# Inverse roots of row and head norms as a power on GpSimd, in place of a root on ScalarE and a reciprocal on VectorE

## The reference

```python
def _layernorm(x, axis=-1, eps=1e-05):
    m = jnp.mean(x, axis=axis, keepdims=True)
    v = jnp.var(x, axis=axis, keepdims=True)
    return (x - m) / jnp.sqrt(v + eps)

# layer A: delta-rule memory with 16 heads of 8, convolutions, two linear scans over time
q = q * jax.lax.rsqrt(jnp.sum(q * q, axis=-1, keepdims=True) + 1e-12)
# layer B: binding in the frequency domain
fk = fk / (jnp.abs(fk) + EPS)

# layer F: causal attention with 16 heads of 8, then 4 experts, 2 chosen per row
def _rms(x, w):
    return x * jax.lax.rsqrt(jnp.mean(x * x, axis=-1, keepdims=True) + EPS) * w
h = _rms(x, n1_w)
q = _rms(heads(wq), qn_w)
k = _rms(heads(wk), kn_w)
...
causal = jnp.tril(jnp.ones((T, T), bool))
```

## Time and profile before

| | us |
|---|---|
| median of 3 runs | 1208.35 (1207.23 to 1209.22) |
| the profiled execution's own time | 1207.07 |
| its span in the trace | 1205.2 |

### The profile page before, as it was taken

The page is one execution under the profiler, slowest core; times in us unless marked ns, Lnnn a source line. Parts: engine busy times, 40 slices in busy tenths (PEclk is TensorE's granted clock), DMA queues, the critical chain, the costliest instruction groups (busy, mean ns, idle before and its releaser), DMA issues.

```text
span 1205.2 us, 11485 instructions
## 1 busy us (share of the span) xinstructions
PE 674.5 (56%) x4014; PEld 333.1 (28%) x4014; DVE 867.5 (72%) x1306; ACT 506.5 (42%) x752; POOL 403.4 (33%) x334
## 2 busy tenths in 40 slices
PE   4990000040004004479899799963264799978997
PEld 2450000040004003222222556631243122225655
DVE  6899999999999995856657733269959557667212
ACT  3423000122220001579999322243034899973321
POOL 1250847600006602226765000006802566650000
PEclk9985555555555556779999799987565899997999
DMA  2250006172000020223310000000003242100001
GB/s 92 70 140 1 1 0 140 35 168 63 13 14 14 0 35 0 84 75 116 97 33 22 1 1 1 1 0 1 0 0 115 63 142 54 54 1 1 1 1 35
DMA packets 30258, 50.71 MB, mean 42 GB/s; under 512 B 4472, under 2 KB 14328, under 8 KB 29176
## 3 DMA queue, kind: packets, MB, share of 16 engines
q1 hardware_dynamic: 29432, 49.32, 15.2%
q10 hardware_dynamic: 768, 0.66, 0.3%
HBM read 20.98 MB, written 16.92 MB: 31 GB/s over the span
## 4 chain that ended last, share of the span: by engine, by line
DVE 47%; PE 23%; ACT 16%; issue 10%; POOL 1%; DMA 1%; ACTq 1%; POOLq 0%; SPq 0%; DVEq 0%
ACT PX L1445 10%; PE PS L1330 6%; PE PS L1308 5%; PE PS L1350 4%; PE PS L1289 3%; DVE D L813 2%; DVE S L817 2%; DVE P L814 2%; DVE PS L871 2%; DVE PRD L870 2%; DVE mag L1031 2%; DVE PA L772 2%; ACT P L688 2%; DVE RO L837 2%; DVE RP L832 2%
## 5 line engine op out<-in xcount | busy, mean ns | idle before, releaser
L1445 ACT ACTIVATE PX<-PS 128x1024 f32<-128x1024 f32 (+1 forms) x320 | 268.1, 1016 | 12.1 <-PE PS L1271 12.1
L1224 POOL TENSOR_TENSOR PX<-PX,maskf 128x256 f32<-128x256 f32 (+1 forms) x192 | 173.4, 931 | 125.0 <-ACT PX L1445 124.5
L1289 PE MATMUL PS<-PX,VA 128*32 128x512 f32 (+3 forms) x1536 | 166.2, 503 | 22.3 <-POOL PX L1224 14.5
L1617 DVE SCALAR_TENSOR_TENSOR X<-PS,wts,X 128x96 f32<-128x96 f32 x128 | 38.4, 315 | 118.2 <-PE PS L1350 103.9
L1271 PE MATMUL PS<-QS,KS 64*128 64x512 bf16 (+3 forms) x768 | 107.8, 339 | 16.7 <-issue 11.4
L1554 DVE RECIPROCAL DEN<-DEN 128x512 f32<-128x512 f32 x32 | 107.3, 3353 | 1.1
L580 PE MATMUL PS<-ones,HT 64*128 64x1 f32 x64 | 13.0, 348 | 152.0 <-ACT HT L672 152.0
L947 POOL TENSOR_TENSOR PRQ<-PA,LQK 128x2048 f32<-128x2048 f32 (+15 forms) x16 | 39.9, 2520 | 151.8 <-DMA WS<-S 138.6
L1552 DVE LOAD_MASK_SELECT DEN<-PS x32 | 0.4, 14 | 107.2 <-PE PS L1289 93.5
L591 PE MATMUL PS<-awout,V 64*128 64x128 f32 x64 | 13.3, 422 | 110.5 <-DVE vss L820 110.5
L1308 PE MATMUL PS<-HT,fw 128*128 128x512 f32 x144 | 71.2, 638 | 3.9 <-DVE HG L1584 2.6
(11 more groups left out here) (264 smaller groups left out, 1649.5 us busy)
## 6 DMA issues: line engine op xcount, KB each, us to landing
QS<-qs_d SPq DMA_DIRECT2D x32, 196.0 KB
qs_d<-QP SPq DMA_DIRECT2D x24, 256.0 KB, 3.9
ks_d<-QP SPq DMA_DIRECT2D x24, 256.0 KB, 4.0
KS<-ks_d SPq DMA_DIRECT2D x32, 192.0 KB
K<-LQK SPq DMA_DIRECT2D x16, 256.0 KB
W<-WS SPq DMA_DIRECT2D x16, 256.0 KB, 4.1
qkv_d<-CY SPq DMA_DIRECT2D x3, 1024.0 KB, 3.9
LQK<-qkv_d SPq DMA_DIRECT2D x8, 256.0 KB, 4.9
```

Source lines behind the costliest of these rows:

```text
L1224: pool.tensor_tensor(block, block, bcast(maskf[:], 1, 2 * halves), ALU.mult).then_inc(probs_masked, 1)
L1289: last = pe.matmul(PS[32 * h:32 * h + 32, SCORES_BANKS + qc, c0:CH], VA[b][:, kt, h, :], px[:, i % 2, at:at + CH - c0], start=(kt == 0), s ...
L1445: act.activation(tile(PX[u % PDEPTH][:]), tile(PS[:, k:k + 2, :]), ACT.Exp).then_inc(probs_ready, 1)
```

## The change

Two semaphores are added: `to_power` from VectorE to GpSimd and `powered` back. For the norm ahead of all four layers, for q and k and the score bound in both F layers, and for the norm ahead of the experts, the request goes to GpSimd, which writes `stat ** -0.5` (or `qst ** 0.5` for the bound) with one `tensor_tensor` of the operation `pow`; the exponent is a value of the new tile `HALVES`, repeated. ScalarE's roots and VectorE's reciprocals at these places go. The roots of `SS`, `vss`, `SS4` and `mag` stay as they were.

```diff
+        HALVES = sb("HALVES", [P, 2])
...
         def dve_norm(v, link, ans, eps, dst, rms_eps=None):
 
-            v.tensor_scalar(stat[:], mv[:, :, 1], eps, None, ALU.add).then_inc(to_act, 1)
+            v.tensor_scalar(stat[:], mv[:, :, 1], eps, None, ALU.add).then_inc(to_power, 1)
             ans.wait()
-            link(v.reciprocal(rstd[:], stat[:]))
...
+        def pool_power(pool, ask, dst, src, exponent):
+            ask.wait()
+            pool.tensor_tensor(dst, src, exponent, ALU.pow).then_inc(powered, 1)
...
-        def a_gpsimd(pool, link):
+        def a_gpsimd(pool, link, pask):
+            link.open(pool.memset(HALVES[:, 0:1], -0.5))
+            link(pool.memset(HALVES[:, 1:2], 0.5))
             pool.memset(ones[:], 1.0).then_inc(ones_set, 1)
+            pool_power(pool, pask, rstd[:], stat[:], bcast(HALVES[:, 0], 1, TILES))
...
-        def b_gpsimd(pool, link):
+        def b_gpsimd(pool, link, pask):
+            pool_power(pool, pask, rstd[:], stat[:], bcast(HALVES[:, 0], 1, TILES))
...
-        def f_gpsimd(pool, link, nth, rep):
+        def f_gpsimd(pool, link, pask, nth, rep):
+            pool_power(pool, pask, rstd[:], stat[:], bcast(HALVES[:, 0], 1, TILES))
+            pool_power(pool, pask, rrms[:], stat[:], bcast(HALVES[:, 0], 1, TILES))
             if rep == 0:
...
+            def unit_power(b):
+                tb = slice(b * TB, (b + 1) * TB)
+                pool_power(pool, pask, qst2[:, tb], qst[:, tb], bcast(bcast(HALVES[:, 0], 1, 2 * H), 1, TB))
+
+            def root(b):
+                at = qst[:, b * TB:(b + 1) * TB, H:2 * H]
+                pool_power(pool, pask, at, at, bcast(bcast(HALVES[:, 1], 1, H), 1, TB))
+
+            unit_power(0)
+            root(0)
+            unit_power(1)
             for c in range(NCH // B):
                 pool.wait_ge(psum_read, FIRST_RESULT[nth] + NCH + TILES + 2 + 2 * (c + 1))
                 third(pool, c).then_inc(third_parts, 1)
+            root(1)
...
+            for b in range(B):
+                tb = slice(b * TB, (b + 1) * TB)
+                pool_power(pool, pask, rrms[:, tb], stat[:, tb], bcast(HALVES[:, 0], 1, TB))
...
             def q_k_normed(b):
...
-                ans.wait()
-                link(v.reciprocal(qst2[:, tb], qst[:, tb]))
+                pans.wait()
                 link(v.tensor_tensor(to, qk, bcast(qst2[:, tb], 3, HD), ALU.mult))
...
-                v.tensor_scalar(stat[:, tb], stat[:, tb], 1.0 / D, F_EPS, ALU.mult, ALU.add).then_inc(to_act, 1)
-                ans.wait()
-                link(v.reciprocal(rrms[:, tb], stat[:, tb]))
+                v.tensor_scalar(stat[:, tb], stat[:, tb], 1.0 / D, F_EPS, ALU.mult, ALU.add).then_inc(to_power, 1)
+                pans.wait()
```

More of the change, by code:

```diff
@@ L264, in hybrid_kernel @@
         to_act = sem("to_act")
+        to_power = sem("to_power")
+        powered = sem("powered")
         normed = sem("normed")
@@ L396, in dve_norm @@
                 link(v.tensor_tensor(var[:], var[:], rstd[:], ALU.mult))
-                v.tensor_scalar(stat[:], var[:], rms_eps, None, ALU.add).then_inc(to_act, 1)
+                v.tensor_scalar(stat[:], var[:], rms_eps, None, ALU.add).then_inc(to_power, 1)
                 ans.wait()
-                link(v.reciprocal(rrms[:], stat[:]))
                 link(v.tensor_tensor(rrms[:], rrms[:], rstd[:], ALU.mult))
@@ L605, in a_scalar @@
         def a_scalar(act, link, ask, reads):
-            act_sqrt(act, ask, stat[:])
             act_ht(act, reads)
@@ L701, in hybrid_kernel, with a_vector @@
         READ_TURNS = [(0,), (1, 2), (3, 4), (5, 6), (7, 8, 9), (10, 11), (12, 13), (14, 15)]
-        def a_vector(v, link, ans):
+        def a_vector(v, link, ans, pans):
             v.wait_ge(x_loaded, 48)
             dve_stats(v, link, range(TILES))
-            dve_norm(v, link, ans, LN_EPS, XL)
+            dve_norm(v, link, pans, LN_EPS, XL)
             v.wait_ge(a_loaded, 112)
@@ L1010, in b_scalar, with b_vector @@
                     act_sqrt(act, ask, mag[c % 2][0:NB])
-        def b_vector(v, link, ans, nth):
+        def b_vector(v, link, ans, pans, nth):
             v.wait_ge(x_ready, nth)
-            dve_norm(v, link, ans, LN_EPS, XL)
+            dve_norm(v, link, pans, LN_EPS, XL)
             v.wait_ge(normed, B * (FIRST_NORM[nth] + 1))
@@ L1397, in f_scalar @@
                 act.activation(QKV[:, t, :], PS[:, k, 0:3 * D], ACT.Copy).then_inc(psum_read, 1)
-                if t == TB + TPC - 1:
-                    act_sqrt(act, ask, qst[:, 0:TB])
             def q_squares(b):
@@ L1403, in q_squares @@
                 act.activation(QQ[b], QKS[:, b * TB:(b + 1) * TB, 0:D], ACT.Square).then_inc(q_squared, 1)
-            def q_root(b):
-                act_sqrt(act, ask, qst[:, b * TB:(b + 1) * TB, H:2 * H])
             def high(c):
@@ L1422, in f_scalar @@
             high(0)
-            q_root(0)
             high(1)
-            act_sqrt(act, ask, qst[:, TB:2 * TB])
             shifts(0)
@@ L1431, in f_scalar @@
             high(2)
-            q_root(1)
             high(3)
@@ L1446, in f_scalar @@
             for b in range(B):
-                act_sqrt(act, ask, stat[:, b * TB:(b + 1) * TB])
                 act_ht(act, reads, range(b * (NCH // B), (b + 1) * (NCH // B)), HT_BANKS)
@@ L1473, in w_vector, with f_vector @@
             link(v.tensor_scalar(fqk[:, 0], fqk[:, 0], HD ** -0.5, None, ALU.mult))
-        def f_vector(v, link, ans, nth, rep):
+        def f_vector(v, link, ans, pans, nth, rep):
             base = FIRST_RESULT[nth]
@@ L1479, in f_vector @@
                 v.sem_inc(o_read, OBANKS)
-            dve_norm(v, link, ans, LN_EPS, SQ, F_EPS)
+            dve_norm(v, link, pans, LN_EPS, SQ, F_EPS)
             def q_k_squares(b):
@@ L1486, in q_k_squares @@
                 link(v.tensor_reduce(qst[:, tb], to, AX.X, ALU.add))
-                v.tensor_scalar(qst[:, tb], qst[:, tb], 1.0 / HD, F_EPS, ALU.mult, ALU.add).then_inc(to_act, 1)
+                v.tensor_scalar(qst[:, tb], qst[:, tb], 1.0 / HD, F_EPS, ALU.mult, ALU.add).then_inc(to_power, 1)
             def q_k_normed(b):
@@ L1505, in q_k_normed @@
                 v.tensor_reduce(qst[:, tb, H:2 * H], QQ[b].rearrange("p t (h d) -> p t h d", d=HD),
-                                AX.X, ALU.add).then_inc(to_act, 1)
-                ans.wait()
+                                AX.X, ALU.add).then_inc(to_power, 1)
+                pans.wait()
                 link(v.tensor_scalar(qst[:, tb, H:2 * H], qst[:, tb, H:2 * H], HD ** 0.5, -SHIFT, ALU.mult, ALU.add))
@@ L1687, in _ @@
         def _(v):
-            link, ans = Chain(v, dve_chain), Tally(v, to_dve)
+            link, ans, pans = Chain(v, dve_chain), Tally(v, to_dve), Tally(v, powered)
             for n, layer in enumerate(LAYERS):
                 if layer == "A":
-                    a_vector(v, link, ans)
+                    a_vector(v, link, ans, pans)
                 elif layer == "B":
-                    b_vector(v, link, ans, n)
+                    b_vector(v, link, ans, pans, n)
                 else:
-                    f_vector(v, link, ans, n, LAYERS[:n].count("F"))
+                    f_vector(v, link, ans, pans, n, LAYERS[:n].count("F"))
         @block.gpsimd
         def _(pool):
-            link = Chain(pool, pool_chain)
+            link, pask = Chain(pool, pool_chain), Tally(pool, to_power)
             for n, layer in enumerate(LAYERS):
                 if layer == "A":
-                    a_gpsimd(pool, link)
+                    a_gpsimd(pool, link, pask)
                 elif layer == "B":
-                    b_gpsimd(pool, link)
+                    b_gpsimd(pool, link, pask)
                 else:
-                    f_gpsimd(pool, link, n, LAYERS[:n].count("F"))
+                    f_gpsimd(pool, link, pask, n, LAYERS[:n].count("F"))
 def dft_tables():
```

## The result

The changed kernel takes 1470.52 us (median of 4 runs, 1469.73 to 1471.05), the kernel before 1208.78 on the same chip: ratio 1.2166, 95% interval 1.2145 to 1.2187, slower by 262 us. The profiled execution has a span of 1467.8 us. Forecast were 1238.9 and a range of 1202 to 1345.

What follows compares the result with a forecast made beforehand. VectorE holds nearly half the chain, and norms it waits for lie on the path. Savings of 14.81 us, collisions of 5.39 and powers of 39.9 gave +30.5 us, 1238.9 us in the runs' terms; range 1202 to 1345.

Steps and rivals of the forecast that it cites:

- 14.8 us of savings: Roots, reciprocals and hand-overs leaving the path at row norms, q, k, score bound and experts' norm: 14.81 us less.
- the price: GpSimd's power at every moved place: 25.3 ns per element, together 39.9 us added to the path.
- The upper bound of 164 ns: Per-element ceiling for the GpSimd power, from its dearest small two-input instruction, 2.807 us for 16 elements: 1468 us.
- The memsets: First F layer: held back behind the powers, they give back 2.29 us, then collide with sixteen scalings, costing 7.2 us.
- Layer B's table load: Layer B: ScalarE's load only moves, ahead of the root of `mag`; 1.28 us comes back, net saving 2.28 us.
- The load after the attention: ScalarE's table load after the attention goes; it costs nothing now, since ScalarE is idle 10.7 us after it.
- rival 4: Two of eighteen table loads go and matter more than the chain shows: 1236.3 us, or 1233.6; chance 0.03.
- Sequence 1 of q and k: F layers: power of 256 beside 2.37 us of subtractions, adding 2 x (6.67 - 2.37) = 8.6 us; 3.38 us saved.
- The norm ahead of the experts in sequence 1: Ahead of the experts: lies beside TensorE's products with about 1 us of cover left, so counted as nothing.
- Rival 3: Power far dearer, above 90 ns per element, as an unpipelined chain of steps: 1345 us and up; chance 0.14.
- Rival 1: Power at the product's rate, kernel faster: 1204.0 us, or 1196.8 without the memset collision; chance of faster 0.15.
- rule on a chain of dependent operations: GpSimd power: 4 cycles per element and operation; 25.3 ns means under eight steps, twenty steps would make +99 us.

Runs made afterwards that it cites:

- product kernel: The changed kernel with the power replaced by a product on GpSimd, same tiles, order and waits: 1211.28 us against 1206.24 before, ratio 1.0041.
- the trace without the collision: The changed kernel with products for powers, the first F layer's six memsets also waiting for the sixteen scalings: 1205.15 us, ratio 0.9993 to the kernel before.
- pricing kernel: The kernel before plus small GpSimd powers and one product on their own tiles, in the pause after layer A's first products: one timed run, 1209.23 us.

## Why the prediction was wrong

The direction was right, the mechanism too (the power's price against 14.8 us of savings), and one term was mis-sized.

**The step that failed** is the price: "I take that value; it is nearer to the product than to the dearest row, as the only rows about arithmetic are". It was 25.3 ns per element, built from a reciprocal's ratio to a product on VectorE; it measures 159 ns, over six times that. What a reciprocal costs beside a product on VectorE said nothing of a power on GpSimd. The upper bound of 164 ns gave 1468 us, and the time came out at 1470.5; that is luck, since the row behind it was a product of 0.24 us, held up to 2.81. But no row of the trace placed the power anywhere, and ending the range at 90 ns had no row behind it either. An operation that the trace does not hold could only be given with a much wider range, or timed first.

With the measured durations the prediction's own sum is -14.8 + 5.4 + 6 x 2.90 + 2 x 41.12 + 4 x 20.72 + 2 x 1.64 + 2 x (41.12 - 2.37) = +254. Measured 262. The sum thus holds once the price is right. The other steps:

- The memsets: predicted 2.29 back and 7.2 lost; found 0.18 us for the epsilon and 10.77 for the scalings, 6.6 lost. Right, and confirmed by moving them (6.1 us).
- Layer B's table load came back onto the chain with its 1.28 us, as predicted. The load after the attention went (16 loads for 18) and bought nothing visible (from the attention's first product to its last shuffle 0.6 us more, not less): rival 4 falls.
- Sequence 1 of q and k: the 2.37 us of cover were right, and against 41 us worth little. The norm ahead of the experts in sequence 1 is not hidden at 1.64 us; the prediction left it out at its own price of 0.39.
- Missed: GpSimd's wait for all copies of QKV, which stood ahead of the first power in the program. 2.7 us in each F layer locally.
- Missed in the other direction: between the last subtraction and the first attention product the first F layer took 523.59 - 515.93 = 7.7 us before and 655.15 - 650.57 = 4.6 after: 3.1 us given back there. As the program reads, TensorE waits there for the transfers of the stacks, which after the long powers had ended; no run tests it.
- The third parts now start together with the scaling of q and k instead of 1.6 us ahead of it, and that instruction takes 4.21 us; before it took 2.7.
- The savings were about right, stage by stage. The product kernel's trace has the row norm of the first F layer 2.8 us shorter up to its first scaling (sum: 2.9), layer B 1.7 (sum: 2.1), and q and k, with the overlooked wait, 0.5 and 0.2 (sum: 0.2 each). What it has above the sum are the products for q, k and v of the first F layer, 13.04 us for 10.59.

Rival 3 was the right one. Rival 1 had the price and the collision as its conditions; with both granted the kernel ties: the overlooked wait takes 5.4 us of it, and in the trace without the collision TensorE's products in layer A and at q, k and v of both F layers take 6.4 us more than in the kernel before.

The Trainium skill's rule on a chain of dependent operations ("GPSIMD Engine Reference", "Performance pitfalls for Q7 kernels") had been weighed on the right side: by its 4 cycles, 3.3 ns, a step, 159 ns would be an estimated 48 steps. No run here shows the steps themselves.

## What to carry to other kernels

An operation that no row of the trace shows should be timed by itself before it goes on the path: one extra instruction in a pause gives the price. A move to an idle engine pays only where the work behind the wait is longer than the operation there; here VectorE asked and waited at once at nearly every place, so GpSimd's idle time was worth nothing. Before a gain of 2 us is read from a stage, look at the same stage in traces of other kernels that leave it alone. And what stands behind a newly waiting instruction in its queue starts exactly when the waiting engine resumes: put it elsewhere if the two collide.

## What the runs showed of the hardware

- The power on GpSimd: 159 ns per element per partition plus some 0.3 us from 8 to 256 elements, against 0.35 us for a whole product of 32 elements. For 32 elements it took 5.42 to 5.99 us over the exponents and bases tried, and the same on 16 partitions as on 128.
- GpSimd's powers do not hold up VectorE. In the pricing kernel 60 us of powers ran beside layer A's work of VectorE, and its tensor_scalar and tensor_tensor took what they took without them within 0.1 us (0.69 us, and 2.32 for 2.29), while a memset of 1.80 us held up a tensor_scalar of 0.17 to 1.84. The collision that the prediction reckons with is thus the memset's and the product's, not the power's. A power with real cover costs VectorE next to nothing: that kernel's one timed run is 1209.23, inside the spread of the kernel before beside it (1201.41 to 1210.46).
- A GpSimd product can itself be held up: the one of 16 elements took 2.81 us beside VectorE's products of 3072 elements and 0.24 us later.
- A root and a reciprocal of 16 values cost 0.51 us with their hand-over the earlier trace rows; there was little to win at the start.
- The same 32 products of TensorE took 10.59 us at a mean granted clock of 1.00 and 13.01 at 0.81, in two traces with the same code in that stage and the same idle time before it.
